# The first attention of a two-layer block on one core: a pipeline of rounds rearranged

## The reference

```
n = layernorm(x)
q, k, v = n @ wq + bq, ctx @ wk + bk, ctx @ wv + bv      # 16 heads of 8
p = softmax(q k^T / sqrt(8)) per head
x = x + (p v) @ wo + bo
x = x + (two of 8 experts, chosen by layernorm(x) @ gate^T, weighted)
x = x + (second attention: 16 heads of 64, low-rank parts, extra tokens)
x = x + (routed network of 16 experts)
```

## Time and profile before

| what | value |
|---|---|
| time, three runs | 512.45 us median (512.03, 512.45, 515.22) |
| the profiled execution's own time | 515.36 us |
| its span | 513.5 us |
| busy: PE, PEld, DVE, ACT, POOL | 94%, 74%, 70%, 56%, 46% |
| chain that ended last: PE, DVE | 79%, 13% |

### The profile page before, as it was taken

The page is one execution under the profiler, slowest core; times in us unless marked ns, Lnnn a source line. Parts: engine busy times, 40 slices in busy tenths (PEclk is TensorE's granted clock), DMA queues, the critical chain, the costliest instruction groups (busy, mean ns, idle before and its releaser), DMA issues.

```text
span 513.5 us, 13588 instructions
## 1 busy us (share of the span) xinstructions
PE 484.3 (94%) x5109; PEld 379.7 (74%) x5113; DVE 357.6 (70%) x1008; ACT 288.3 (56%) x984; POOL 234.9 (46%) x331
## 2 busy tenths in 40 slices
PE   3799999999999999999999999899989999999996
PEld 2557676756667777877878877778757898899995
DVE  5778889766676876657865757657976879635553
ACT  3265655554377776667666677556774544513332
POOL 4753545126364446556456653433421891090440
PEclk9999999999899999999999999999999999999999
DMA  8810000000001001110000000022100300000001
GB/s 231 199 35 4 3 3 3 3 1 8 4 0 33 6 29 34 34 33 25 11 3 3 3 3 1 1 64 65 48 17 9 118 0 1 2 20 25 1 2 42
DMA packets 21872, 14.48 MB, mean 28 GB/s; under 512 B 5928, under 2 KB 21136, under 8 KB 21808
## 3 DMA queue, kind: packets, MB, share of 16 engines
q1 hardware_dynamic: 20704, 13.31, 9.5%
q10 hardware_dynamic: 1104, 0.30, 0.3%
HBM read 12.30 MB, written 1.05 MB: 26 GB/s over the span
## 4 chain that ended last, share of the span: by engine, by line
PE 79%; DVE 13%; ACT 2%; issue 2%; DMA 2%; ACTq 1%; DVEq 0%
PE bank L1813 9%; PE bank L1742 6%; PE bank L1822 5%; PE bank L1570 5%; PE bank L1577 5%; PE bank L1529 5%; PE bank L1557 5%; PE bank L1393 5%; PE bank L1482 5%; PE bank L1549 4%; PE bank L1540 4%; PE bank L1378 3%; PE bank L1829 3%; DVE work L789 2%; DVE negmax L779 2%
## 5 line engine op out<-in xcount | busy, mean ns | idle before, releaser
L1169 ACT ACTIVATE work<-bank,negmax 128x124 f32<-128x124 f32 x256 | 90.0, 387 | 54.0 <-DVE ipa_s L781 53.9
L504 POOL TENSOR_TENSOR work<-work,rsum 128x496 f32<-128x496 f32 x64 | 64.1, 1012 | 122.8 <-DVE rsum L795 122.8
L539 POOL TENSOR_SCALAR work<-work,slot 128x128 f32<-128x128 f32 x64 | 50.2, 799 | 44.7 <-DVE slot L870 25.8
L1169 ACT ACTIVATION_READ_ACCUMULATOR work<-bank,negmax 128x1 f32 x256 | 58.9, 230 | 0.0
L1813 PE MATMUL bank<-work 128*128 128x256 f32 x224 | 53.4, 381 | 0.0
L1321 ACT ACTIVATE work<-bank 128x256 f32<-128x256 f32 x64 | 24.5, 383 | 40.9 <-PE bank L1813 30.4
L1032 DVE SCALAR_TENSOR_TENSOR work<-work,bank 128x256 f32<-128x256 f32 x64 | 26.8, 419 | 28.7 <-ACT work L1321 28.5
L487 POOL TENSOR_TENSOR work<-work 128x512 f32<-128x512 f32 (+2 forms) x48 | 39.2, 818 | 12.1 <-DVE work L751 9.6
L312 DVE TENSOR_TENSOR x_all<-bank,x_all 128x128 f32<-128x128 f32 x16 | 4.7, 291 | 56.9 <-PE bank L1742 54.8
L1813 PEld LDWEIGHTS bank<-work 128*128 128x128 f32 x224 | 40.3, 190 | 4.7 <-DVE work L1035 0.2
L438 POOL TENSOR_TENSOR rstd<-veps,minus_half 128x1 f32<-128x1 f32 (+3 forms) x28 | 21.2, 755 | 47.2 <-DVE veps L581 47.1
(11 more groups left out here) (199 smaller groups left out, 1103.2 us busy)
## 6 DMA issues: line engine op xcount, KB each, us to landing
work<-in_L_ffn_w_dram SPq DMA_DIRECT2D x42, 128.0 KB, 2.3
x_all<-in_x_dram SPq DMA_DIRECT2D x4, 256.0 KB, 5.3
out_dram<-x_all SPq DMA_DIRECT2D x4, 256.0 KB, 2.5
ctx_all<-in_ctx_dram SPq DMA_DIRECT2D x4, 192.0 KB, 6.2
ctx_all<-in_L_ffn_w_dram SPq DMA_DIRECT2D x6, 128.0 KB, 2.4
work<-in_L_xattn_Wq_dram SPq DMA_DIRECT2D x1, 512.0 KB, 6.2
work<-in_L_xattn_Wo_dram SPq DMA_DIRECT2D x1, 512.0 KB, 7.0
work<-in_L_ffn_We_dram SPq DMA_DIRECT2D x1, 512.0 KB, 6.0
```

The lines of the kernel that those rows point to most:

```text
L504: pool.tensor_tensor(part, part, rsum1[:, b % 2, CH * n:CH * n + CH].unsqueeze(2).broadcast_to((128, CH, ORG)), ALU.mult).then_inc(Z.norm, 1)
L539: ins = pool.tensor_scalar(ohw_of(e)[:, k, :], count[:, :], slot[:, h, 0, k, e % E1:e % E1 + 1], slot[:, h, 1, k, e % E1:e % E1 + 1], ALU. ...
L1169: ins = act.activation(p1[:, b % 2, n, c, 0:ORG], blocks(bank[n])[:, c, 0:ORG], ACT.Exp, bias=negmax1[:, b % 2, h:h + 1], accum_out=sums1[ ...
```

## The change

The rounds run from -3 to B + 2 on PE, DVE and ACT. Transposition is b + 3, K/Q/V b + 2, both maxima b + 1 (first maxima before, second after the scores), turn b, values b - 1, projection b - 3 (from round 15 on the last ones: 12 and 13 in round 15, 14 in 16, 15 in 17). PE's order in a steady round: turn, projection, transposition, K/Q/V, first maxima, picks and scores, second maxima, values. The turn goes to bank 4 and is copied by ACT, the projection to bank 5 (13 to bank 2, 14 and 15 to bank 7). Products come after round 0, the bias is added from round 1 on; K/Q/V waits for three loads, the biases have semaphores of their own and wv is loaded fifth. On DVE the gate's logits and shares of batches 0 to 3 follow the residuals of round 15, and the later work on the experts moves by one round. POOL does its masked copies first in a round. What follows is the core; the rest renumbers rounds.

```diff
@@ banks
+        NEGMAX_TO = bank[4][:, 0:128]
+        def projected_in(b):
+            return (b - 3,) if b < B - 1 else (B - 4, B - 3) if b == B - 1 else (b - 2,)
+        def project_to(y):
+            return (bank[5] if y < B - 3 else bank[2] if y == B - 3 else bank[7])[:, 0:128]
@@ DVE
+            def round0(b):
+                m, t, y = b + 1, b - 2, projected_in(b)[0]
+                if there(t):
+                    summed0(t)
+                if b < B and there(y):
+                    residual0(y)
+                if there(t):
+                    normalised0(t)
+                if b >= B and there(y):
+                    residual0(y)
+                if there(m):
+                    maxima0(m, 1 if b <= 0 else 0)
+                if there(y):
+                    statistics0(y)
+                if b == 15:
+                    head_logits(0, bank[0])
+                for y in projected_in(b)[1:]:
+                    residual0(y)
+                    statistics0(y)
...
+                if b < 0 and there(m + 1):
+                    maxima0(m + 1, 0)
...
+                if b > 0 and there(m):
+                    maxima0(m, 1)
                 if b in (11, 12):
                     head_input(0, 2 * (b - 11), 2 * (b - 10))
...
+            for b in range(-3, B + 3):
                 round0(b)
-                if b == -4:
+                if b == -1:
                     product_input()
-                if b == -3:
+                if b == 0:
                     products_taken()
...
-                if b == 14:
+                if b == 15:
                     head_weights(0)
-                if b >= 15:
-                    weighted(b - 15, bank[3])
+                if b >= 16:
+                    weighted(b - 16, bank[3])
@@ ACT
-            for w, name in ((wk0, "wk"), (wq0, "wq"), (wv0, "wv")):
+            for w, name in ((wk0, "wk"), (wq0, "wq")):
                 act.dma_start(w[:, :], T["L0_xattn_" + name]).then_inc(got.qkv0, 16)
-            for bias, name in ((bk0, "bk"), (bq0, "bq"), (bv0, "bv")):
+            for bias, name in ((bk0, "bk"), (bq0, "bq")):
...
+            act.dma_start(wv0[:, :], T["L0_xattn_wv"]).then_inc(got.qkv0, 16)
...
+                if there(b):
+                    act.wait_ge(A.negT, b + 1)
+                    act.activation(negmax0T[:, b % 2, :], NEGMAX_TO, ACT.Copy).then_inc(A.negT_sb, 1)
                 if there(c):
                     act.wait_ge(A.qkv, c + 1)
@@ PE
+                after(pe, A.exp, min(2 * b - 1, 2 * B))
+                if there(b):
+                    turn0(b)
+                if b < B and there(projected_in(b)[0]):
+                    project0(projected_in(b)[0])
                 if there(a):
                     pe.wait_ge(A.xn, a + 1)
+                    after(pe, A.xT, a)
+                    after(pe, A.vm, c)
                     pe.transpose(TURN0[:, 0:128], xn_in[:, a % 3, :], ident[:, :]).then_inc(A.tr, 1)
...
+                if b == -2:
+                    turn_ctx(1)
+                if b == 15:
+                    head_logits(0, bank[0])
                 if there(m):
+                    maxima0(m, 1 if b <= 0 else 0)
+                if b == -1:
+                    turn_ctx(2)
...
+                if there(b):
+                    after(pe, A.x_new, b - 2)
+                    scores0(b)
+                if b < 0 and there(m + 1):
+                    maxima0(m + 1, 0)
+                if b > 0 and there(m):
+                    maxima0(m, 1)
+                if b == -1:
+                    turn_ctx(3)
+                if b >= B:
+                    pe.wait_ge(A.exp, 2 * B)
+                    after(pe, A.x_new, b - 2)
+                    if there(b - 2):
+                        project0(b - 2)
                 if there(t):
                     values0(t)
+                if b == B - 1:
+                    project0(B - 3)
...
+            for b in range(-3, B + 3):
+                if b == 14:
                     pe.wait_ge(A.vm, B)
                     head_turn(0, bank[0])
+                if b >= 16:
+                    if b == 16:
+                        pe.wait_ge(A.x_new, B - 2)
+                        pe.wait_ge(got.ffn0, 16)
+                    after(pe, F.ys0, b - 16)
+                    ffn(b - 16, 0, bank[2])
...
                 round0(b)
-                if b == -3:
+                if b == 0:
                     products()
...
-                if b == 14:
+                if b == 15:
                     pe.wait_ge(F.step, 1)
                     down_turn()
-                if b == 15:
-                    pe.wait_ge(A.x_new, 14)
+                if b == 16:
+                    pe.wait_ge(W.downT, 3)
                     fold(0)
```

More of the change, by code:

```diff
@@ L541, in slot_rows @@
                 ins.then_inc(X1.ohw, 1)
-            for b in range(-4, B - 1):
+            for b in range(-3, B):
                 round0(b)
@@ new lines, in round0 @@
+            def round0(b):
+                m, t, y = b + 1, b - 2, projected_in(b)[0]
[16 more added lines that the diff above has]
+                    statistics0(y)
+                if b < 0 and b > -3:
+                    xn0_of(b + 4)
+                if -3 <= b <= -2:
+                    rstd_at["first", b] = first_statistics(4 * (b + 4), 4 * (b + 5), x_in[b + 4])
+                if b < 0 and there(m + 1):
+                    maxima0(m + 1, 0)
+                if b == -1:
+                    rstd_at["first", b] = first_statistics(4 * (b + 4), 4 * (b + 5), x_in[b + 4])
+                if b in (0, 4, 8):
+                    dve.wait_ge(ln.rstd, rstd_at["first", b // 4 - 3])
+                if b >= 0 and there(b + 4):
+                    xn0_of(b + 4)
+                if b > 0 and there(m):
+                    maxima0(m, 1)
@@ L680, in round0 @@
                 if b in (11, 12):
                     head_input(0, 2 * (b - 11), 2 * (b - 10))
[L682 to L688, removed]
@@ L1104, in round0 @@
                         .then_inc(A.vm, 1)
+                if b == -2:
+                    context_turned(1)
+                if b == -1:
+                    context_turned(2)
+                    context_turned(3)
                 if there(b):
@@ L1291, in round1 @@
                     values(f, 1)
-            for b in range(-4, B + 2):
-                if b == 13:
+            for b in range(-3, B + 3):
+                if b == 14:
                     head_turned(0, bank[0])
[L1295 to L1299, removed]
+                round0(b)
+                if b == 15:
                     head_powers(0)
                     down_turned()
-                if b >= 15:
-                    weighted(b - 15, bank[2])
-                if b == 15:
+                if b >= 16:
+                    weighted(b - 16, bank[2])
+                if b == 16:
                     take(0)
-                if b == 16:
+                if b == 17:
                     take(1)
@@ L1386, in values0 @@
                 pe.wait_ge(A.vm, t + 1)
-                if t + 1 < FILL:
-                    after(pe, A.negT_sb, min(t + 3, B))
-                    after(pe, A.x_new, t)
+                after(pe, A.o, t)
+                if t == 0:
+                    pe.wait_ge(made.bias, 1)
+                    pe.wait_ge(F.gateT, 1)
                 for part, of in ((0, vm0[:, t % 5, :, :]), (128, own_col)):
```

212 lines of the change are left out of this document (68 added, 144 removed).

## The result

The changed kernel takes 515.03 us (median of 20 runs, 513.3 to 517.49), the kernel before 512.69 beside it (20 runs, 511.33 to 515.66): a ratio of 1.004 [1.0025, 1.0054]. The forecast was 512.0, no change; the time is inside the range and within 1%, but it moved by 0.4% the other way.

What follows compares the result with a forecast made beforehand. The prediction took PE, busy 94% of the span, as the bound. Fill -6.0, twelve rounds +1.2 and tail +4.3 gave -0.5; put on the median of 512.45 this made 512.0 us, range 507 to 517.

Steps and rivals of the forecast that it cites:

- fill, to the values of batch 1: Start of the first attention: fewer load waits and an earlier clock rise bring values of batch 1 6.0 us earlier.
- twelve rounds: Steady rounds, batch 1 to 13: PE waits 0.24 to 0.34 for the first reduction, 5.31 a round; 1.2 us lost.
- tail: From values of batch 13 to the second attention's first input: 1.65 more PE work plus a 2.6 wait, 4.3 lost.
- It lies 2.9 above the median of the timed runs, 512.45, and the change is put on the median: Final sum: profiled execution 515.36, by the sum 514.86; set against the median of the timed runs, giving 512.0 us.
- 31.7: Fill: forecast start of the values of batch 1, against 37.74 in the profiled kernel before, a gain of 6.0.
- The clock falls in the tail: Rival, chance 0.12: the 2.6 wait in the tail lowers PE's clock, costing 1.7 more, 513.7 us.
- upper bound of +4.2: Twelve rounds: upper bound of the loss, taken from the rival in which the reduction starts late.
- DVE arrives in time: Steady round: DVE finishes reciprocal, residual and normalisation by about 67.7, 0.1 before the first maxima end at 67.83.
- both waits are covered: Rival, chance 0.2: the waits in the steady rounds and the tail are covered; sum -7.2, 505.2 us.
- the reduction starts late: Rival, chance 0.15: DVE's residual holds up the reduction 0.25 to 0.35 each steady round; 515 to 516.2 us.

Runs made afterwards that it cites:

- e2: The changed kernel with three more expert-product matmuls, read by nobody, in PE's wait for the normalisation of batch 14: 512.87 us, ratio 1.0032 to the kernel before.
- e8: The changed kernel with GpSimd's masked keys behind its masked queries from batch 4 on: 513.61 us, one execution.
- e1: The changed kernel with the gate's ties and beats before batch 13's residual on DVE, shares behind batch 14's normalisation: 509.99 us, ratio 0.9956 to the kernel before.

## Why the prediction was wrong

The account, in us, by the marks of the prediction; the right column pairs the two profiled executions whose times lie nearest the medians (512.44 and 514.28).

| term | forecast | profiled pair | pair near the medians |
|---|---|---|---|
| fill, to the values of batch 1 | -6.0 | -7.5 | -4.0 |
| twelve rounds | +1.2 | +1.0 | +1.0 |
| tail | +4.3 | +5.4 | +5.6 |
| behind the first input | 0 | +3.2 | -0.8 |
| sum | -0.5 | +2.1 | +1.8 |

The last column comes near what the many runs give (515.03 - 512.69 = 2.3). Of the -0.8, 0.6 are a wait in the second attention that is 0.62 long in the execution of 512.44 and absent in the other; no run tells why. The size of the loss is less sure than its sign: the kernel before, in five sets of 11 to 29 runs, has medians from 512.34 to 514.11, all below 515.03.

**The step that failed is "It lies 2.9 above the median of the timed runs, 512.45, and the change is put on the median".** The gain of the fill was measured from an execution whose extra length lay in that very fill. Its wait of 1.89 for the output weights (the row names the output bias, which the same wait covers), one of the two waits that the prediction named in the fill, is 0 to 0.43 in the three other executions. A kernel that no longer has that wait gains it only against the executions that do: between the two near the medians the fill is worth 4.0 (4.9 and 5.3 if the other two stand for the kernel before). The forecast's own mark, 31.7, against these three (34.77 to 36.10) is a gain of 3.1 to 4.4 and not 6.0, and with it its sum is +1.1 to +2.4: the sign is right. Its mark for the first input, near 120, was met (119.34 and 120.03); in the kernel before this lies at 117.42, 118.34 and 118.76, and at 120.40 only in the execution that was read.

**The second is the place of the rival "The clock falls in the tail", given 0.12.** Mechanism and price were right (1.7 forecast, 1.4 to 1.7 measured, e2), but by the profiles it belonged to the forecast's own step: the profile had shown a fall behind a wait of 1.06, and the forecast itself put a wait of 2.6 there.

Point by point otherwise:

- *Fill:* every mark to the first picks within 0.25; the values came 1.1 and 1.4 earlier than forecast, with the clock up 2 us sooner.
- *Round:* 5.31 forecast, 5.32 measured, but that near only by luck. From the first to the second maxima it is 1.80 for 1.71, because PE starts 0.14 behind the end of the reduction where the forecast took 0.06. The rest of the round was put too high: without the collision below a round makes 5.23 (e8), so 3.43 for 3.60. The other 0.09, some 0.9 in all, is that collision of DVE and GpSimd, which no step had and e8 removes. (The upper bound of +4.2 leaves out the forecast's own 1.2; with it, it is 5.4. Nothing rests on it.) The forecast's sentence that DVE arrives in time looked only at the first reduction. The Trainium skill (SBUF — State Buffer, Who interferes with whom) says that a tensor_scalar can, if its operands allow, use a pair of ports that DVE shares with GpSimd, and that whoever issues first holds it for the whole instruction while the other is blocked. The row of the changed kernel agrees: it begins 0.05 behind GpSimd's and ends 0.08 behind its end. In e8 it overlaps the last 0.24 of GpSimd's and is no longer for it, so there the rows do not show the block: that the two collide is shown, by which ports is not.
- *Tail:* the wait was 2.79 for 2.6 and its releaser as named; turn, projection, logits and what else is more in the tail cost 0.9 for 1.65 (21.31 in e1, which has neither wait nor low clock there, for 20.40).
- *Rivals:* "both waits are covered" fell with the first steady round, "the reduction starts late" with the row of the reduction, where DVE has stood idle for 0.31 until the maxima came, so nothing in its queue held it up.

## What to carry to other kernels

A gain that is read from one execution must be put against the same stretch of other executions before it is put on a median: the stretch in which the executions differ is the one in which the edit will gain less (here 4 for 7.5). A wait put at PE where there was none costs its length and, as the 2.79 here, can cost a stretch of low clock behind it, so the two go into the sum together. And when work moves, compare the mean length of every unmoved instruction, view by view: 0.38 turned into 0.99 in one line, and a reordering of two independent products on another engine took it back (0.35).

## What the runs showed that was not expected

The kernel before, run against itself, came out 0.24% slower [0.01%, 0.47%]. The same instruction (128x128 f32, DVE's normalised input) takes 0.33 or 1.07 depending on when GpSimd's product of 128x512 starts beside it. The releaser that the profile names can be a bystander: GpSimd's keys ended 0.04 before the second maxima started, and moving them changed nothing of the wait. The granted clock fell at the 2.8 wait in every profile that has it (six of six), behind the wait of 1.06 in twelve of fourteen profiles and behind the one of 1.15 in two, but in none behind the waits of 0.28.
